# Rows of a source tile's first four blocks taken by one-hot products on TensorE in a graph network's two tile passes

## Chip, cores and metric

One core of a Trainium2 chip runs one program. The metric is the device time of one execution in microseconds, as the median of three runs.

## What is computed

Four graph layers follow each other on 6,250 nodes of 128 numbers and 100,000 edges. The edges come sorted by `dst`, and their `src` is random. The change touches the last two layers, which take the graph the other way round: they sum over `src` and read rows at `dst`.

```python
# third layer: dst = edge_index[0], src = edge_index[1], edge_index = stack([src, dst]);
# h = relu(layernorm(x)) is the feature
feat_n = feature[src] * relation_weight
seg_sum = segment_sum(feat_n, dst, n)
seg_cnt = segment_sum(ones, dst, n)
neigh_mean = seg_sum / maximum(seg_cnt, 1.0)
x = x + concatenate([feature, neigh_mean]) @ W + b
# fourth layer: row, col = edge_index; deg counts row; h = relu(layernorm(x))
agg = segment_sum(deg_inv_sqrt[row] * deg_inv_sqrt[col] * h[col], row, n)
x = x + agg @ W.T + b
```

## The kernel before

A node tile is 128 nodes, and there are T = 49 of them. `edge_layout`, `histogram`, `order_nodes`, `lay_runs` and `place_edges` build the lists for the first two layers. The first layer is four `edge_pass` loops ("attend"), the second one more ("heads"), and in both GpSimd gathers rows with indirect DMAs.

While the first three edge passes run, a sort in their shadow writes the edges to `regions_d` in DRAM: one region for each source tile (`src >> 7`), and in it, edge after edge, one word that packs the table row of `dst` with the place of `src` in its tile, and in a second region the edge's weight. `list2_setup` prepares this sort from edges laid out as [128 partitions x 816 columns] in `so.store`. `place_rest` ends it and leaves in `chunks` how many chunks of 2,176 edges the fullest tile needs, which is one here.

`norm_rows` writes the normalised rows to `table_d` and keeps them in SBUF as `k.q`. Then `tile_pass` runs twice, as "weigh" (third layer) and as "sum" (fourth layer). For each source tile it handles 2,176 edges as GC = 17 columns of 128:

- GpSimd (POOL) issues 17 indirect DMAs, each of which gathers 128 rows into `rows[b]` (L1269). There are RB = 4 such buffers, so it may be up to four tiles ahead of the sums.
- VectorE (DVE) compares `order` (in PSUM) with the edges' places and gets the tile's 17 one-hot matrices (L1366).
- ScalarE (ACT), in the "weigh" pass alone, multiplies each column's rows by the edge weights (L1407). In the "sum" pass the rows are used as they are.
- TensorE (PE) sums the 17 products of one-hot matrix and rows in `total` in PSUM (L1470), which DVE adds to `k.sums` (L1278).

Every eight tiles a group is finished: PE transposes (L1431), multiplies (L1441, L1446, L1451), DVE and ACT normalise, SP stores. Every engine runs its own program in order, and the engines wait for each other's semaphores. The first gather of the "sum" pass needs the last rows that the "weigh" pass stored. SP issues the plain DMAs: the packed lists (L1244) and the stores.

## Time and profile before

| What | us |
|---|---|
| Median of three runs | 11020.37 |
| The three runs | 11018.97, 11020.37, 11024.36 |
| Span of the profiled execution, first to last instruction | 8504.6 |

The profiled execution's own time is not given apart from the runs. The runs' median is 2515.8 us above its span; that part lies around the instructions, where the profile shows nothing. In the span, POOL is busy for 69%, DVE for 42%, PE for 40% and ACT for 26%. The two tile passes take the last 2,143 us of the span. "PEclk" and "granted clock" are the share of TensorE's full clock, 0.50 (1.2 GHz) or 1.00 (2.4 GHz). A float32 matmul stands in the trace as two MATMUL records, so the 17 products of a tile are 34 records. The time of an indirect DMA on POOL is that of writing its descriptors; the transfer comes behind it.

### The profile page before, as it was taken

What the parts mean: (1) busy time and instruction counts of PE and PEld (TensorE: products, weight loads), DVE (VectorE), ACT (ScalarE), POOL (GpSimd) and SP (SyncE); (2) the same over time, 40 slices, a digit from 0 to 9 for tenths busy, and PEclk for the clock granted to TensorE, in tenths of its full rate; (3) what the DMA queues carried; (4) which work ended last, traced back from release to release, by engine and by line L of the source; (5) the groups of instructions that cost most, each with busy time, mean ns of one, the idle gap of its engine ahead of it and who ended that gap; (6) DMA issues with size and microseconds to landing.
All of it is one profiled execution on the core that took longest, in us unless ns stands there. A gap on an engine that the chain in (4) does not pass through costs nothing. (4 is left out here: it accounts for less than half of the span.)

```text
span 8504.6 us, 106528 instructions
## 1 busy us (share of the span) xinstructions
PE 3426.3 (40%) x18282; PEld 3028.2 (36%) x18283; DVE 3575.8 (42%) x13136; ACT 2245.1 (26%) x6884; POOL 5889.8 (69%) x6182
## 2 busy tenths in 40 slices
PE   5434443444434344434333354454542333323333
PEld 4234443444434344434322342333322333323233
DVE  7455553455533555433333355777751111111111
ACT  0212222322223222223222233555532222200000
POOL 0467777577776777766777746777747777677777
PEclk9566666666667666667666677777766666666666
DMA  0322222122221222211222213333322222122222
GB/s 21 93 48 53 54 54 55 42 53 54 53 54 43 51 54 53 54 49 49 54 54 54 55 40 110 105 105 105 105 70 54 55 58 55 53 55 58 55 55 55
DMA packets 374250, 509.70 MB, mean 60 GB/s; under 512 B 217568, under 2 KB 259556, under 8 KB 373796
## 3 DMA queue, kind: packets, MB, share of 16 engines
q0 software_dynamic: 212288, 464.41, 20.5%
q1 hardware_dynamic: 149854, 38.28, 2.1%
q10 hardware_dynamic: 11978, 5.55, 0.3%
q8 instruction: 49, 0.80, 0.0%
q14 instruction: 81, 0.66, 0.0%
HBM read 458.78 MB, written 49.00 MB: 60 GB/s over the span
## 5 line engine op out<-in xcount | busy, mean ns | idle before, releaser
L1625 POOL DMA_INDIRECT rows<-table_d,meta x3200 | 3035.5, 949 | 1013.2 <-issue 894.2
L1685 PE MATMUL ps_total<-weighted_rows,ident 128*128 128x129 f32 (+1 forms) x8000 | 1733.8, 397 | 2495.8 <-ACT weighted_rows L1708 2006.7
L1685 PEld LDWEIGHTS ps_total<-weighted_rows,ident 128*128 128x128 f32 x8000 | 1558.3, 275 | 2665.2 <-issue 2556.5
L1827 DVE SCALAR_TENSOR_TENSOR prod<-rows,q_rows 128x129 f32<-128x129 f32 x3200 | 928.5, 294 | 2120.4 <-DMA rows<-table_d,meta 1584.0
L1470 PE MATMUL tile_sums<-tile_rows,sums 128*128 128x129 f32 x3332 | 609.7, 366 | 1504.8 <-ACT tile_rows L1407 766.4
L1470 PEld LDWEIGHTS tile_sums<-tile_rows,sums 128*128 128x128 f32 x3332 | 592.4, 279 | 1524.5 <-issue 1510.6
L1269 POOL DMA_INDIRECT tile_rows<-table_d,tile_halves x833 | 789.9, 948 | 266.3 <-issue 253.6
L1269 POOL DMA_INDIRECT tile_rows<-rows_d,tile_halves x833 | 789.3, 948 | 265.4 <-issue 253.7
L1708 ACT ACTIVATE weighted_rows<-rows,power 128x129 f32<-128x129 f32 x3200 | 959.4, 389 | 6.5
L1625 POOL DMA_INDIRECT rows<-pairs_d,meta x800 | 774.9, 969 | 257.9 <-issue 243.2
L1702 ACT ACTIVATE power<-expo 128x17 f32<-128x17 f32 x200 | 43.6, 218 | 3020.9 <-DVEq L1860 3020.9
L1278 DVE TENSOR_TENSOR sums<-sums,tile_sums 128x129 f32<-128x129 f32 x98 | 28.4, 290 | 1728.4 <-PE tile_sums L1470 1728.4
L1719 ACT ACTIVATE weighted_rows<-once_weighted,of_relation 128x136 f32<-128x136 f32 x1600 | 484.7, 393 | 191.7 <-DVE once_weighted L1879 190.0
L1407 ACT ACTIVATE tile_rows<-tile_rows,tile_packed 128x128 f32<-128x128 f32 x833 | 248.8, 387 | 787.1 <-DMA tile_rows<-table_d,tile_halves 787.1
L1662 PE MATMUL sort_made<-sort_to_slot,sort_to_tile 128*98 128x80 f32 x1728 | 283.6, 360 | 235.4 <-DVEq L1804 235.4
L1662 PEld LDWEIGHTS sort_made<-sort_to_slot,sort_to_tile 128*98 128x98 f32 x1728 | 274.3, 273 | 245.8 <-DVEq L1804 245.8
L1830 DVE TENSOR_TENSOR src_store<-rows,q_rows 128x128 f32<-128x128 f32 x800 | 211.1, 289 | 257.9 <-DMA rows<-pairs_d,meta 256.7
L1377 ACT COPY sums<-tile_turned 128x1024 f32<-128x1024 f32 (+2 forms) x21 | 18.7, 892 | 1058.0 <-PE tile_turned L1431 1058.0
L1827 DVE DVE_READ_ACCUMULATOR prod<-rows,q_rows 128x1 f32 x3200 | 262.9, 82 | 0.0
L2402 POOL DMA_INDIRECT table_d<-h_rows,perm_in x147 | 147.6, 1004 | 146.0 <-DVE h_rows L2371 102.1
L1366 DVE TENSOR_TENSOR sums<-tile_order,tile_packed 128x2176 f32<-128x2176 f32 x98 | 237.4, 2425 | 12.6 <-DVE x_rows L1319 1.2
L1643 PE MATMUL ps_total<-nothing,ident_bf 128*128 128x129 bf16 (+1 forms) x780 | 105.1, 250 | 312.5 <-issue 226.6
(569 smaller groups left out, 4756.8 us busy)
## 6 DMA issues: line engine op xcount, KB each, us to landing
rows<-table_d,meta POOLq DMA_INDIRECT x3200, 2.5
tile_rows<-table_d,tile_halves POOLq DMA_INDIRECT x833, 2.5
tile_rows<-rows_d,tile_halves POOLq DMA_INDIRECT x833, 2.5
rows<-pairs_d,meta POOLq DMA_INDIRECT x800, 2.8
meta<-list_in_d SPq DMA_DIRECT2D x250, 32.0 KB
words<-words_in_d SPq DMA_DIRECT2D x250, 0.0 KB
resets<-resets_in_d SPq DMA_DIRECT2D x250, 8.0 KB
table_d<-em_h ACTq DMA_DIRECT2D x7, 448.0 KB, 4.7
```

The source lines that it names most:

```text
L1269: pool.indirect_dma_start(rows[b][:, c, 0:P], None, table_d, bass.IndirectOffsetOnAxis(meta[:, t, c:c + 1], 0)).then_inc(got[b] if t < T - ...
L1366: dve.tensor_tensor(spare[:, q], order[:].unsqueeze(1).to_broadcast([P, GC, P]), lane_no[:, t, :].unsqueeze(2).to_broadcast([P, GC, P]), A ...
L1407: ins = act.activation(rows[b][:, c, 0:P], rows[b][:, c, 0:P], ACT.Copy, scale=packed[:, 1, t, c:c + 1])
L1470: mm = pe.matmul(total[:, q, 0:P + 1], spare[:, q, c, :], rows[t % RB][:, c, :], start=(c == 0), stop=(c == GC - 1))
L1625: pool.indirect_dma_start(rows[q][:, j, 0:width], None, table_d, bass.IndirectOffsetOnAxis(meta[q][:, j, number:number + 1], 0)).then_inc( ...
L1662: pe.matmul(placed_ps, to_tile[:, c].rearrange("p r t -> p (r t)"), to_slot[:, c, :], start=(c == 0), stop=(c == SC - 1), skip_group_check ...
L1685: mm = pe.matmul(total[:, q, ds(part, 1), 0:W].rearrange("p a w -> p (a w)"), k.ident[:], wide[:, j % WS, :], start=False, stop=True, skip ...
L1708: ins = act.activation(wide[:, j, :], rows[q][:, j, :], ACT.Copy, scale=power[q][:, 0, j + 1:j + 2])
L1719: ins = act.activation(wide[:, j % WS, r * HW:(r + 1) * HW], once[:, j].rearrange("p h d -> p (h d)"), ACT.Copy, scale=of_relation[q][:, j ...
L1827: own(dve.scalar_tensor_tensor(prod[:, j, :], rows[q][:, j, :], -1.0, asked, ALU.mult, ALU.mult, accum_out=score[:, j, :]))
L1830: own(dve.tensor_tensor(prod[:, j, :], rows[q][:, j, 0:w], asked, ALU.mult))
L2402: pool.indirect_dma_start(k.table_d, bass.IndirectOffsetOnAxis(k.perm[:, t:t + 1], 0), k.h[:, t, :], None).then_inc(m["scattered"], 16)
```

## The change

The first four of the 17 columns of each source tile (its first 512 edges) no longer come from GpSimd. Since edges reach the regions in order of `dst`, the table rows of such a column all lie in a few node tiles, a window: columns 0 to 3 read tiles 0 to 4, 2 to 7, 4 to 10 and 7 to 14. For each of the 5 + 6 + 7 + 8 = 26 node tiles in the windows, DVE makes a one-hot matrix and PE multiplies it with the table's tile in SBUF, 26 float32 products, which leave the column's rows in PSUM (`gathered`). ACT copies them to SBUF ("sum") or weighs them on the way ("weigh"). POOL issues FARC = 13 indirect DMAs instead of 17.

What goes with it:

- `edge_layout` and `histogram` load the edges a second time, in their natural order, straight into `so.store` (six DMAs on SP beside the histogram, in pieces of 64 bytes). `list2_setup` works from these.
- A new stage, `near_edges`, behind `place_rest`, splits the near columns' words into window row and place, and stores both. Edges outside their window would go to a second list, and `sweeps` would then be 2: both tile passes would run all tiles twice.
- The tables must be in SBUF: `k.q` in "weigh", and the rows that "weigh" makes now go to `k.x` instead of the two buffers `made`. What stood in `k.x` is read back from `rows_d` (`residual`, one DMA of all rows). The "sum" pass gathers from a new `made_d`.
- SP loads for each tile the window rows of its 512 near edges, spread over all partitions (`rows_of_window`).

```diff
-PARTS = (0, 6, 11, 15, 17)
+PARTS = (0, 5, 9, 12, 13)
+WINDOWS = ((0, 5), (2, 6), (4, 7), (7, 8))
+NEAR = len(WINDOWS)
+FARC = GC - NEAR
+BATCHES = ((0, 3), (1, 2))
+HOTS = 3
 # GpSimd
-                        for c in range(GC):
+                        for c in range(FARC):
                             pool.indirect_dma_start(rows[b][:, c, 0:P], None, table_d, ...
 # VectorE
+                    def spread_windows(t):
+                        dve.wait_ge(windowed[t % 2], 16 * (t // 2 + 1))
+                        for i, columns in enumerate(BATCHES):
+                            n = len(BATCHES) * t + i
+                            if n >= HOTS:
+                                dve.wait_ge(m["gathered"], n - HOTS + 1)
+                            at = 0
+                            for c in columns:
+                                w = WINDOWS[c][1]
+                                ins = dve.tensor_tensor(near_hot[n % HOTS][:, at:at + w, :], window[t % 2][:, c].unsqueeze(1).to_broadcast([P, w, P]),
+                                                        window_of[:, 0:w].unsqueeze(2).to_broadcast([P, w, P]), ALU.is_equal)
+                                at += w
+                            ins.then_inc(m["near_hot"], 1)
...
+                            if t + 1 < T:
+                                spread_windows(t + 1)
 # ScalarE
                     for t in range(T + 4):
+                        if t < T:
+                            act.wait_ge(m["gathered"], len(BATCHES) * (t + 1))
+                            if t >= 2:
+                                act.wait_ge(m["summed"], t - 1)
+                            taken = gathered[:, 0:NEARP].rearrange("p (c w) -> p c w", w=P)
+                            if weigh:
+                                for c in range(NEAR):
+                                    ins = act.activation(near_rows[q][:, c, 0:P], taken[:, c, :], ACT.Copy, scale=near[:, 1, t, c:c + 1])
+                            else:
+                                ins = act.copy(near_rows[q][:, :, 0:P], taken)
+                            ins.then_inc(m["near_rows"], 1)
                         if weigh and t < T:
-                                act.wait_ge(got[b], (t // RB + 1) * GC * 16)
-                            for c in range(GC):
+                                act.wait_ge(got[b], (t // RB + 1) * FARC * 16)
+                            for c in range(FARC):
 # TensorE
+                    def gather(t):
+                        if t:
+                            pe.wait_ge(m["near_rows"], t)
+                        for i, columns in enumerate(BATCHES):
+                            n = len(BATCHES) * t + i
+                            pe.wait_ge(m["near_hot"], n + 1)
+                            at = 0
+                            for c in columns:
+                                first, w = (WINDOWS if t < T - 1 else WINDOWS_LAST)[c]
+                                for j in range(w):
+                                    mm = pe.matmul(gathered[:, c * P:(c + 1) * P], near_hot[n % HOTS][:, at + j, :],
+                                                   table[:, first + j, 0:P], start=(j == 0), stop=(j == w - 1), skip_group_check=True)
+                                at += w
+                            mm.then_inc(m["gathered"], 1)
...
+                            pe.wait_ge(m["near_rows"], t + 1)
+                            for c in range(NEAR):
+                                pe.matmul(total[:, q, 0:P + 1], spare[:, q, c, :], near_rows[q][:, c, :], start=(c == 0), stop=False)
                             if t < T - 1 and weigh:
                                 pe.wait_ge(m["weighted"], t + 1)
                             elif t < T - 1:
-                                pe.wait_ge(got[t % RB], (t // RB + 1) * GC * 16)
+                                pe.wait_ge(got[t % RB], (t // RB + 1) * FARC * 16)
...
                             mm.then_inc(m["summed"], 1)
+                        if t + 1 < T:
+                            gather(t + 1)
 # near_edges, the engines' work in one turn, shortened
+                    for r in range(2):
+                        sp.dma_start(listed[:, r].rearrange("t c p -> t (c p)"), so.regions_d[r * T:(r + 1) * T, ds(e * CHUNK, NEARP)]
+                                     ).then_inc(m["listed"], 16)
...
+                    own(dve.tensor_copy(whole[:], listed[:, 0]))
+                    own(dve.tensor_scalar(real[:], listed[:, 0], 0.0, None, ALU.is_lt))
...
+                    for c in range(NEAR):
+                        pe.transpose(facts_ps[:, 0, c, 0:T], lane[:, c, :], k.ident[0:T, 0:T])
+                        mm = pe.transpose(facts_ps[:, 1, c, 0:T], listed[:, 1, c, :], k.ident[0:T, 0:T])
...
+                    sp.dma_start(so.near_d[ds(e, 1)].rearrange("a p f -> (a p) f"), facts[:].rearrange("p r t c -> p (r t c)")
+                                 ).then_inc(m["stored"], 16)
+                    sp.wait_ge(m["stored"], 5 * 16)
```

On TensorE in the "weigh" pass, from the fifth source tile on, a tile was one row of 17 products (`tile_sums` is `total`, `tile_turned` and `tile_new` are the group's transposes and products):

```order
L1470 MATMUL tile_sums<-tile_rows_13920,sums 128x129 x17
L1470 MATMUL tile_sums<-tile_rows_13921,sums 128x129 x17
L1470 MATMUL tile_sums<-tile_rows_13922,sums 128x129 x17
L1431 MATMUL tile_turned<-ident,q_rows 128x128 x8
L1470 MATMUL tile_sums<-tile_rows_13923,sums 128x129 x17
L1441 MATMUL tile_new<-bias_parts_3299,ones_bf 128x512 x6
L1446 MATMUL tile_new<-w_3295,sums 128x128 x8
```

The same tiles in the changed kernel (`near_gathered` is `gathered`, `q_rows` the table, and `near_rows` and the window rows lie in `src_store`):

```order
L1698 MATMUL tile_sums<-src_store,sums 128x129 x4
L1708 MATMUL tile_sums<-tile_rows_14218,sums 128x129 x13
L1684 MATMUL near_gathered<-q_rows,near_hot_14225 128x128 x13
L1684 MATMUL near_gathered<-q_rows,near_hot_14226 128x128 x13
L1698 MATMUL tile_sums<-src_store,sums 128x129 x4
L1708 MATMUL tile_sums<-tile_rows_14219,sums 128x129 x13
L1684 MATMUL near_gathered<-q_rows,near_hot_14224 128x128 x13
L1684 MATMUL near_gathered<-q_rows,near_hot_14225 128x128 x13
```

Each tile's 17 products are now in two pieces, and the next tile's 26 gather products stand behind them, ahead of any group work.

On ScalarE in the "weigh" pass, around the first group's transposes, it was:

```order
L1407 ACTIVATE tile_rows_13922<-tile_rows_13922,tile_packed 128x128 x17
L1407 ACTIVATE tile_rows_13923<-tile_rows_13923,tile_packed 128x128 x17
L1377 COPY sums<-tile_turned 128x1024
L1407 ACTIVATE tile_rows_13920<-tile_rows_13920,tile_packed 128x128 x17
L1407 ACTIVATE tile_rows_13921<-tile_rows_13921,tile_packed 128x128 x17
```

And in the changed kernel:

```order
L1626 ACTIVATE tile_rows_14220<-tile_rows_14220,tile_packed 128x128 x13
L1614 ACTIVATE src_store<-near_gathered,src_store 128x128 x4
L1626 ACTIVATE tile_rows_14221<-tile_rows_14221,tile_packed 128x128 x13
L1586 COPY sums<-tile_turned 128x1024
L1614 ACTIVATE src_store<-near_gathered,src_store 128x128 x4
L1626 ACTIVATE tile_rows_14218<-tile_rows_14218,tile_packed 128x128 x13
```

The weighing of a tile's 13 gathered columns now stands behind the four that read what TensorE gathered for the same tile.

On VectorE, per tile, one comparison of 2,176 elements became two of together 2,176, followed by four that make the next tile's window matrices:

```order
L1571 TENSOR_TENSOR sums<-tile_fixed,src_store 128x512
L1573 TENSOR_TENSOR sums<-tile_fixed,tile_packed 128x1664
L1548 TENSOR_TENSOR near_hot_14225<-src_store,tile_fixed 128x640
L1548 TENSOR_TENSOR near_hot_14225<-src_store,tile_fixed 128x1024
L1548 TENSOR_TENSOR near_hot_14226<-src_store,tile_fixed 128x768
L1548 TENSOR_TENSOR near_hot_14226<-src_store,tile_fixed 128x896
```

`tile_fixed` is in PSUM and holds both `order` and `window_of`; the other operand is in SBUF.

## Rows read from the trace of the kernel before

**Rows 1.** The page: the span, and each engine's busy time, share and instructions.

```profile
span 8504.6 us, 106528 instructions
PE 3426.3 (40%) x18282; PEld 3028.2 (36%) x18283; DVE 3575.8 (42%) x13136; ACT 2245.1 (26%) x6884; POOL 5889.8 (69%) x6182
```

**Rows 2.** The chain that ended last, from 7300 us on: share by line.

```profile
by line: POOL tile_rows L1269 65.3%; issue 21.1%; DMA tile_rows<-rows_d,tile_halves 0.2%; DMA tile_packed<-list_out_d 0.2%; PE tile_new L1451 0.1%; PE tile_sums L1470 0.1%; POOLq L1239 0.1%; PE tile_new L1441 0.1%; PE tile_turned L1431 0.1%
```

**Rows 3.** Line 1269: instructions (ns min/median/max, first and last start us) and idle.

```profile
L1269 POOL DMA_INDIRECT tile_rows<-table_d,tile_halves x833: 941/947/1561, 6375.3 to 7417.9; - x167
L1269 POOL DMA_INDIRECT tile_rows<-rows_d,tile_halves x833: 940/947/1569, 7449.0 to 8490.9; - x167
  issue: 507.3, 1664
```

**Rows 4.** Waits of the whole span: who waited, us, times, longest.

```profile
PE tile_sums L1470 <- ACT tile_rows L1407: 766.4, 50, 92.3
PE tile_sums L1470 <- DMA tile_rows<-rows_d,tile_halves: 738.5, 52, 43.3
```

**Rows 5.** Timeline of a tile in "weigh": start, us, engine, line, count, idle before.

```profile
6716.83 5.07 ACT L1407 ACTIVATE tile_rows<-tile_rows,tile_packed 128x128 f32<-128x128 f32 x17 [15.92 <-DMA tile_rows<-table_d,tile_halves]
6721.81 0.99 ACT L1377 COPY sums<-tile_turned 128x1024 f32<-128x1024 f32 x1
6722.04 5.67 PE L1470 MATMUL tile_sums<-tile_rows,sums 128*128 128x129 f32 x34 [14.20 <-ACT tile_rows L1407]
```

**Rows 6.** Timeline of PE at the start of a tile's products.

```profile
6701.05 4.13 PE L1470 MATMUL tile_sums<-tile_rows,sums 128*128 128x129 f32 x18 [15.05 <-ACT tile_rows L1407]
```

**Rows 7.** Windows: us, busy of PE, PEld, DVE, ACT, POOL, PEclk, DMA, GB/s.

```profile
6701.00:6704.90 3.90, 3.85 (x18) 3.88 (x19) 0.00 (x0) 0.00 (x0) 2.99 (x4) 0.50 0.23 61
6729.00:6730.00 1.00, 1.00 (x9) 0.96 (x9) 1.00 (x2) 0.00 (x0) 0.69 (x2) 1.00 0.23 66
```

**Rows 8.** Timeline of "weigh" around a group's work on DVE and PE.

```profile
6728.64 1.23 DVE L1311 TENSOR_TENSOR sums<-sums,tile_inv 128x1024 f32<-128x1024 f32 x1
6729.05 2.05 PE L1446 MATMUL tile_new<-w,sums 128*128 128x128 f32 x16
6729.37 1.31 POOL L1269 DMA_INDIRECT tile_rows<-table_d,tile_halves  x1 [0.30 <-issue]
6729.78 2.42 DVE L1366 TENSOR_TENSOR sums<-tile_order,tile_packed 128x2176 f32<-128x2176 f32 x1
6730.99 0.94 POOL L1269 DMA_INDIRECT tile_rows<-table_d,tile_halves  x1 [0.30 <-issue]
```

**Rows 9.** Timeline of ACT and DVE in the layer turn: work on 512 columns.

```profile
5001.62 0.57 ACT L2306 COPY lt_ht<-lt_rows 128x512 f32<-128x512 f32 x1
5000.26 0.69 DVE L2384 TENSOR_TENSOR x_rows<-x_rows,lt_out 128x512 f32<-128x512 f32 x1
```

**Rows 10.** Timeline of `place_rest`: its first and last steps, and the next stage's first.

```profile
5010.85 0.48 PE L1050 MATMUL rest_turned<-ident,sort_base 98*1 98x98 f32 x2 [2.29 <-PEq L94]
5015.63 1.87 DVE L1102 MEMSET rest_blank<- 98x2176 f32 x1 [2.13 <-DVEq L1104]
5023.82 0.15 DVE L1127 CAST rest_idx<-rest_place 128x1 int32<-128x1 f32 x1 [3.75 <-DMA list_out_d<-sort_lane]
5039.90 0.53 POOL L2493 MEMSET hw_mix<- 128x512 f32 x1 [8.75 <-DMA list_out_d<-rest_rec,rest_idx]
```

**Rows 11.** Lines from 0 to 175 us (busy us, mean ns): the histogram's products.

```profile
L256 PE MATMUL hist_count<-oh 128*128 128x49 bf16 x784 | 90.0, 277 | 14.5 <-DVE oh L226 14.5
```

**Rows 12.** DMA issues: count, KB each, median us to landing.

```profile
x_rows<-rows_d SPq DMA_DIRECT2D x7, 448.0 KB, 6.7
tile_packed<-list_out_d SPq DMA_DIRECT2D x28, 59.5 KB, 3.3
```

More of the change, by code:

```diff
@@ L1206, in tile_pass @@
         if weigh:
-            made = [buf(nc, s, f"tile_made{q}", [P, TG, P]) for q in range(2)]
             stats = buf(nc, s, "tile_stats", [P, TG, 6])
@@ L1220, in tile_pass @@
         parts = k.parts2 if weigh else k.parts3
+        table = k.q if weigh else k.x
         turns = nc.values_load(chunks[0:1, 0:1], min_val=1, max_val=CHUNKS)
+        again = nc.values_load(sweeps[0:1, 0:1], min_val=1, max_val=2)
         TURNS_OF = 2 if weigh else 1
@@ L1237, in _ @@
                     dve.memset(rows[b][:, :, P:P + 1], 1.0)
-        with nc.Fori(0, turns) as e:
+                for q in range(2):
+                    dve.memset(near_rows[q][:, :, P:P + 1], 1.0)
+        with nc.Fori(0, turns) as e, nc.Fori(0, again) as again_i:
             with nc.Block() as block:
```

258 lines of the change are left out of this document (210 added, 48 removed).

## The prediction

> **What bounds the kernel now.** I read the page first: no engine is busy throughout, but POOL is far ahead with 69% [rows 1]. Then I asked the chain that ended last for the stretch of the two tile passes. The reader is to see there that nearly all of it is POOL's line 1269 and the "issue" behind it [rows 2]: one indirect DMA after another, with 0.3 us between them. So the passes last as long as POOL needs for its gathers. Line 1269's own view gives the pace [rows 3]: 833 gathers start from 6375.3 to 7417.9 us in "weigh" and from 7449.0 to 8490.9 us in "sum", that is 1042.6 / 832 = 1.253 us and 1041.9 / 832 = 1.252 us each. A tile of 17 costs 21.3 us. It hardly ever waits for anyone else: the idle time of the two passes is 507.3 us of "issue" in 1664 pieces, which is the 0.3 us that belongs to each gather. The waits say the same from the other side [rows 4]: PE stands idle some 15 us per tile, for ACT in one pass (766.4 us) and for the DMA in the other (738.5 us). What a change is worth here is read from POOL's count of gathers, as long as no other loop gets longer than POOL's.
>
> **What is removed.** 4 x 49 = 196 gathers a pass, 392 in all. At 1.253 us that is 245.6 us a pass, **-491 us** in all. POOL's tile then takes 13 x 1.253 = 16.3 us.
>
> **What takes its place, and whether it hides under 16.3 us.** This is the step that I chose most carefully, because in "weigh" the new work closes a ring. PE gathers tile t+1 only behind the sums of tile t; ACT can weigh the 13 gathered columns of t+1 only behind the four that PE's products left in PSUM; and PE can sum the 13 only when ACT is done. In the order above these stand behind each other on either engine. So one tile of "weigh" costs, whatever POOL does:
>
> - on PE 13 sums and 26 gather products, 39 float32 products or 78 records. At half clock a stretch of 3.90 us held 18 records, 3.85 us of work, so 0.214 us each [rows 7]. At full clock 16 records took 2.05 us, 0.128 us each with the tail of the last [rows 8], and a microsecond touches nine; I take 0.12.
> - on ACT 4 + 13 columns: 17 took 5.07 us [rows 5]. The four come out of PSUM; I price them alike.
> - three hand-offs: ACT ended at 6721.90 and PE began at 6722.04, 0.14 us each [rows 5], 0.4 us.
>
> At full clock throughout this is 9.4 + 5.5 = 14.9 us; at half clock 16.7 + 5.5 = 22.2 us. Which of the two? In the trace PE comes out of 15 us of idle, does 18 records in 4.13 us at half clock [rows 6], and is at full clock afterwards [rows 7, 8]. In the new loop a burst is 78 records long and the pause before it is some 5 us, with four sums (8 records) inside it. If each burst still begins cold, it is 18 x 0.214 + 60 x 0.12 = 11.1 us, and the ring 16.6 us. I take this value, since PE still pauses in each tile: 0.3 us over POOL's 16.3, times 48 tiles, **+15 us**. The ends are 14.9 us (POOL paces, +0) and 22.2 us (+289). The group's own products stand behind the next tile's gather, where PE waits for ACT's 5 us anyway, and ACT's group work (0.99 us for a copy of 1,024 columns [rows 5]) lies under PE's burst: nothing.
>
> In "sum" ACT weighs nothing. The ring is 86 records and one copy of 512 columns, 0.57 us [rows 9], with 0.3 us of hand-offs: 11.2 us at full clock, 3.9 + 68 x 0.12 + 0.9 = 13.0 us when each burst begins cold, 19.3 us at half clock. I take 13.0: POOL paces, nothing is lost. Its bad end is (19.3 - 16.3) x 49 = +147 us.
>
> DVE adds 3,328 compared elements a tile in four instructions. 2,176 took 2.42 us [rows 8], so 3.7 us; with the old comparison and the add it is about 6.7 of 16.3 us. Its window matrices are made a tile ahead in three buffers. If this cover were gone they would stand in the ring at 3.7 us a tile. They could also disturb POOL. The trace shows both sorts: while L1311, with both inputs in SBUF, ran, a gather took 1.31 instead of 0.94 us, and beside L1366, with one input in PSUM, it took 0.94 us [rows 8]. The new ones have one input in PSUM (`window_of`), so I price this at nothing.
>
> [...]
>
> **SP's queue.** Window rows for tile t are fetched as soon as the matrices of t-2 are made, a tile before they are used; a fetch like it takes 3.3 us to land [rows 12], against 16 us. The residual is 3.2 MB; a seventh of it takes 6.7 us to land [rows 12], seven one behind the other at most 47 us. The window rows of tile 2 queue behind it. POOL reaches the end of tile 1 only 33 us into the pass and has four buffers, so this delays at most the second or third tile, once: I take +1 us, and 14 as its end. The stores stand in SP's program six tiles after their group and hold nothing up. Extra constants at each pass's start, 1 us each. Together **+3 us**.
>
> **The new stage.** The trace has no such stage; its nearest relative is `place_rest`, which from 5010.85 to 5039.90 us did 29 us of small steps with two waits for writes to DRAM, of which the last cost 8.75 us [rows 10]. For `near_edges` I count: fills on POOL, one of 3,328 columns (2,176 took 1.87 us [rows 10], so 2.9 us) and some eighteen small ones, 8 us; the lists, 3.3 us; 14 DVE steps of 512 columns at 0.69 us [rows 9], 9.7 us; transposes and their copy, 2 us; the last store and its wait, 8.75 us; the reduction and the barriers of three blocks, 5 us. **+37 us**, ends 20 and 60.
>
> **Nothing for the rest.** The six loads in natural order are 18,750 pieces of 64 bytes. A packed list is 896 pieces of 68 bytes (59.5 KB) and lands in 3.3 us, and 28 of them were loaded without anyone waiting long [rows 12]; the new ones are as much as 21 of them, at worst 69 us one after the other, and lie beside the histogram, whose products alone take 90.0 us [rows 11]. `list2_setup` does three DVE steps fewer but waits for its blank store as before.
>
> **Sum.** -491 + 15 + 3 + 37 = -436 us. It is made against the profiled execution: its span of 8504.6 us becomes 8069 us. Its time apart from the runs' median of 11020.4 us isn't given; I keep the 2515.8 us around the span as they are, and get 10584 us.
>
> **Rivals.**
>
> *TensorE's ring paces.* If PE runs colder than I take it, "weigh" goes to 22.2 us a tile at worst and "sum" to 19.3: 10584 - 15 + 289 + 147 = 11005 us. For it: all of PE's bursts now begin at half clock, and the ring is already equal to POOL's pace. Against: bursts get more than twice as long and pauses three times shorter. A middle case, 0.18 us a record (half the records cold), gives 14.0 + 5.5 = 19.5 us in "weigh" alone, +157 instead of +15: 10726 us.
>
> *DVE's comparisons hold up POOL.* As worked out from the 1.31 us row: 0.36 us for a 1.23 us instruction, so 1.1 us a tile, +106 us, 10690 us; at worst 363 us, 10947 us. Against it is the 0.94 us row.
>
> *The part around the span moves too.* The profile says nothing of these 2515.8 us. If they went with the span, they would shrink by 436 x 2515.8 / 8504.6 = 129 us, 10455 us; if they went with what the program allocates in DRAM, which grows by two more sets of regions and the new tables, they would grow, by a sum that I can't bound from the trace.
>
> *Slower: a second sweep.* One edge outside its column's window is enough for `sweeps` to be 2, and then both passes run all 49 tiles again: 2 x (798 + 31) = 1658 us (31 us lie between the last gather of "weigh" and the first of "sum" [rows 3]), 12242 us. The order within a region decides it, and whether it is truly the order of `dst`. I counted the reference's edges by source tile in that order: all 49 x 512 lie in their windows, and the fullest tile has 2,168 of 2,176 places. So I hold it unlikely. It is also the case in which the change would not do what it says.
>
> **How the numbers follow.** As forecast, POOL or an equal ring pacing, 10540 to 10640 us: 0.63. A colder ring, 10640 to 10900: 0.16. DVE disturbing POOL: 0.04. The part around the span shrinking, 10440 to 10510: 0.07; growing: 0.06, half of it beyond the gain. Second sweep: 0.04. The range from 10510 to 10700 holds the first case, the cheaper half of the second and third, both ends of the new stage. A difference of 0.2%, 22 us, is about what can be told from none here. Faster by more: 0.92; within: 0.02; slower: 0.06 (second sweep, half of the growth, less what overlaps).
>
> **What would show it.** The gather line should have 637 instructions a pass, still 1.25 us apart, and about 798 us from first to last in "sum". In "weigh" POOL should start to wait for PE's sums late in the pass if the ring is longer than 16.3 us; the granted clock of a burst shows which end was right. The port rival would show as gathers over 1 us beside the window comparisons. `near_edges` should last 37 us. The prediction is wrong if "weigh" spans more than 900 us, if the gathers double, or if time and span no longer differ by 2516 us.

## The result, and the profile after

The changed kernel took 10827.82 us (median of four runs, 10819.31 to 10837.80) beside 11022.37 us of the kernel before (four runs, 11018.97 to 11025.45): ratio 0.9826, 95% interval 0.9812 to 0.9840. It is 195 us faster, and I had forecast 436. The cause came out when both kernels ran beside each other on other chips. The forecast's gain was measured on one chip and not on the four others, and by its time the profile of before belongs to the first kind, the timed runs to the second. One execution of the variant e2_again took 10756 us where its four others took 10559 to 10593, and its median below is that of the four.

The page of the changed kernel, the lines that answer to [rows 1]:

```profile
span 10817.6 us, 117700 instructions
PE 4633.8 (43%) x23388; PEld 3788.7 (35%) x23389; DVE 3961.6 (37%) x13646; ACT 2271.5 (21%) x6933; POOL 5523.9 (51%) x5814
```

This execution took 10819.71 us. Its span is 2 us shorter, not 2,516. So nothing lies "around" the instructions: here the 2,516 us are in the span. This was one of the prediction's own signs of being wrong; "weigh" over 900 us, below, is a second. The gathers' line, which answers to [rows 3]:

```profile
L1455 POOL DMA_INDIRECT tile_rows<-table_d,tile_halves x637: 941/947/1306, 8648.8 to 9734.9; - x160
L1455 POOL DMA_INDIRECT tile_rows<-made_d,tile_halves x637: 941/947/1508, 9811.5 to 10772.6; - x160
...
  PE tile_sums L1708: 429.7, 73
  issue: 360.4, 1182
```

There are 637 gathers a pass as forecast, each as long as before (947 ns), but "weigh" lasts 1086.1 us from the first to the last and "sum" 961.1 us, not 798. POOL waits 429.7 us for PE's sums, of which there was nothing in the profile of before. What PE is late for is seen in the timeline of one tile in "sum":

```profile
10316.29 5.97 PE L1684 MATMUL near_gathered<-x_rows,near_hot 128*128 128x128 f32 x52
10319.40 1.95 DVE L1548 TENSOR_TENSOR near_hot<-src_store,tile_fixed 128x768 f32<-128x768 f32 x2 [8.42 <-PE near_gathered L1684]
...
10326.49 0.59 ACT L1616 COPY src_store<-near_gathered 128x512 f32<-128x512 f32 x1 [16.96 <-DMA rows<-table_d,meta]
10326.57 1.95 DVE L1548 TENSOR_TENSOR near_hot<-src_store,tile_fixed 128x640 f32<-128x640 f32 x2 [2.39 <-DMA rows<-table_d,meta]
...
10327.22 2.06 PE L1698 MATMUL tile_sums<-src_store,sums 128*128 128x129 f32 x8 [4.96 <-issue]
```

PE's 52 records end at 10322.26. ACT and DVE, which wait for them alone, start at 10326.49 and 10326.57, some 4.2 us late and at the same moment. (The named releaser is a guess of the profile: that line had issued its last gather 3,800 us earlier.) Over "weigh" this hand-off, from the end of PE's gather burst to ACT's start, has a median of 5.2 us; I had priced each of the three at 0.14. Summed over the 49 tiles of "weigh" these hand-offs take 328 us, and in the trace of a0_fifth (next section) 1.9 us. The gather bursts themselves take 306 us here and 297 there, so it is the hand-off and not the new products that got long.

### The profile page after: what moved, and what is told of

It reads as the page before. It is cut to its first block and busy times, and to the rows that moved or that the text cites. A ratio compares the mean times of both kernels' runs of the same rounds, so it can differ in the third digit from the quotient of the medians.

```text
span 10817.6 us, 117700 instructions
## 1 busy us (share of the span) xinstructions
PE 4633.8 (43%) x23388; PEld 3788.7 (35%) x23389; DVE 3961.6 (37%) x13646; ACT 2271.5 (21%) x6933; POOL 5523.9 (51%) x5814
## 5 line engine op out<-in xcount | busy, mean ns | idle before, releaser
L1925 PE MATMUL ps_total<-weighted_rows,ident 128*128 128x129 f32 (+1 forms) x8000 | 2267.6, 436 | 4384.2 <-issue 3355.9
L1455 POOL DMA_INDIRECT tile_rows<-table_d,tile_halves x637 | 603.8, 948 | 495.3 <-PE tile_sums L1708 303.0
L1548 DVE TENSOR_TENSOR near_hot<-src_store,tile_fixed 128x640 f32<-128x640 f32 (+3 forms) x392 | 381.4, 1016 | 1240.1 <-issue 487.7
L1455 POOL DMA_INDIRECT tile_rows<-made_d,tile_halves x637 | 604.4, 949 | 370.0 <-issue 180.2
L1698 PE MATMUL tile_sums<-src_store,sums 128*128 128x129 f32 x784 | 180.2, 402 | 632.8 <-issue 377.0
L1698 PEld LDWEIGHTS tile_sums<-src_store,sums 128*128 128x128 f32 x784 | 156.2, 295 | 652.4 <-issue 652.4
L1684 PE MATMUL near_gathered<-x_rows,near_hot 128*128 128x128 f32 x2548 | 337.0, 291 | 75.5 <-issue 74.8
L1684 PEld LDWEIGHTS near_gathered<-x_rows,near_hot 128*128 128x128 f32 x2548 | 322.3, 207 | 85.6 <-issue 85.3
L1684 PE MATMUL near_gathered<-q_rows,near_hot 128*128 128x128 f32 x2548 | 299.0, 278 | 74.6 <-issue 74.6
L1684 PEld LDWEIGHTS near_gathered<-q_rows,near_hot 128*128 128x128 f32 x2548 | 295.4, 195 | 75.0 <-issue 74.9
```

What stands on the lines that cost most here:

```text
L1455: pool.indirect_dma_start(rows[b][:, c, 0:P], None, table_d, bass.IndirectOffsetOnAxis(meta[:, t, c:c + 1], 0)).then_inc(got[b] if t < T - ...
L1548: ins = dve.tensor_tensor(near_hot[n % HOTS][:, at:at + w, :], window[t % 2][:, c].unsqueeze(1).to_broadcast([P, w, P]), window_of[:, 0:w] ...
L1684: mm = pe.matmul(gathered[:, c * P:(c + 1) * P], near_hot[n % HOTS][:, at + j, :], table[:, first + j, 0:P], start=(j == 0), stop=(j == w ...
L1698: pe.matmul(total[:, q, 0:P + 1], spare[:, q, c, :], near_rows[q][:, c, :], start=(c == 0), stop=False)
L1925: mm = pe.matmul(total[:, q, ds(part, 1), 0:W].rearrange("p a w -> p (a w)"), k.ident[:], wide[:, j % WS, :], start=False, stop=True, skip ...
```

## The same two kernels on the other kind of chip

The page, the gathers and the windows of the changed kernel (a0_fifth) on a chip where the kernel before takes 8,499 us:

```profile
span 8032.8 us, 117700 instructions
PE 3989.1 (50%) x23388; PEld 3571.6 (44%) x23389; DVE 3953.1 (49%) x13646; ACT 2268.3 (28%) x6933; POOL 5509.4 (69%) x5814
```

```profile
L1455 POOL DMA_INDIRECT tile_rows<-table_d,tile_halves x637: 940/944/1739, 6395.9 to 7190.8; - x160
L1455 POOL DMA_INDIRECT tile_rows<-made_d,tile_halves x637: 940/944/1289, 7225.4 to 8019.9; - x160
...
  issue: 387.7, 1272
```

POOL hardly waits for anything but its own 0.3 us, as before the change. Windows of the two passes, columns as in [rows 7] (stretch, its length, PE, PEld, DVE, ACT, POOL, granted clock, DMA share, GB/s):

```profile
6395.90:7190.80 794.90, 613.22 (x4466) 591.57 (x4467) 353.63 (x495) 265.66 (x878) 601.11 (x636) 0.85 0.29 77
7225.40:8019.90 794.50, 606.41 (x4360) 585.47 (x4361) 336.41 (x384) 34.56 (x55) 600.66 (x636) 0.84 0.28 73
```

The kernel before on such a chip (b0_again), its gathers:

```profile
L1269 POOL DMA_INDIRECT tile_rows<-table_d,tile_halves x833: 941/947/1562, 6382.4 to 7425.8; - x167
L1269 POOL DMA_INDIRECT tile_rows<-rows_d,tile_halves x833: 941/947/1983, 7457.1 to 8502.2; - x167
```

From these and the two spans (8515.9 and 8032.8) the difference comes apart:

| Stretch | before, us | changed, us | difference | my term |
|---|---|---|---|---|
| up to the first tile gather | 6382.4 | 6395.9 | +13.5 | +37 |
| "weigh", first to last gather | 1043.4 | 794.9 | -248.5 | -245.6 + 15 |
| between the passes | 31.3 | 34.6 | +3.3 | +3 in all |
| "sum", first to last gather | 1045.1 | 794.5 | -250.6 | -245.6 |
| last gather to end | 13.7 | 12.9 | -0.8 | 0 |
| sum | | | -483.1 | -436 |

The medians are 8499.39 and 8036.40 us, -463 us. (The profiled execution of b0_again took 8517.4.)

What the kinds of chips differ in shows in register steps, the address and counter arithmetic that an engine's own program does between its instructions ("DVEq" for VectorE's), shortest/median/longest in ns. First the kind of a0_fifth, then that of the first comparison, the same line of the same program:

```profile
L2067 DVEq ALU_OP  x6400: 40/45/52, 494.1 to 4914.6; - x194
L2067 DVEq FUSED_REGOPS  x3200: 67/67/80, 494.3 to 4914.7; - x189
```

```profile
L2067 DVEq ALU_OP  x6400: 2/45/1424, 507.8 to 6540.8; - x194
L2067 DVEq FUSED_REGOPS  x3200: 2/67/1424, 508.1 to 6540.9; - x189
```

The median is the same, but there are stretches in which a step takes 0.70 us. In the first comparison's trace I count 5,926 of 34,962 register steps at 0.4 us or more, together 4,290 us: 2,894 on DVE, 2,954 on PE, 78 on SP, none on ACT or POOL; in that of b0_again and a0_fifth not one. They come in phases, as from 994.6 to 1029.2 us, in which DVE and PE are slow from and to the same moment. I call this the crawl. The same line also shows where most of the time lies: the four "attend" passes end their products at 4914.6 us on the one, at 6540.8 on the other, 1,626 of the 2,785 us between the two spans of the changed kernel.

## Experiments

Each group has its own runs of the kernel before on the same chip, so ratios and differences are taken within a group. Groups A and E ran on one and the same chip, 40 minutes apart, without the crawl both times; B, C, D and F ran on four different chips, all with it. So the kind without the crawl is known from one chip, and from the first profile of before. A single run has no ratio.

| Group | before, us | kernel | us | ratio (95%) |
|---|---|---|---|---|
| A | 8497.24 | b0_again (one run) | 8517.44 | |
| | | e1_window_late | 8037.23 | 0.9459 (0.9443 to 0.9474) |
| | | e2_far_first | 8041.54 | 0.9464 (0.9448 to 0.9480) |
| B | 11007.78 | a0_again | 10835.56 | 0.9837 (0.9820 to 0.9853) |
| | | port_window_sbuf | 10916.61 | 0.9914 (0.9893 to 0.9935) |
| | | ring9_near_first | 10665.76 | 0.9689 (0.9669 to 0.9708) |
| | | b13_gathers_only | 10489.53 | 0.9528 (0.9509 to 0.9548) |
| C | 10858.17 | b0_third (one run) | 10856.04 | |
| | | a0_third | 10606.98 | 0.9772 (0.9756 to 0.9788) |
| | | e2_again | 10568.26 | 0.9732 (0.9716 to 0.9748) |
| | | e1_again | 10581.08 | 0.9747 (0.9727 to 0.9766) |
| D | 10992.82 | a0_fourth | 10813.44 | 0.9840 (0.9823 to 0.9856) |
| | | port_again | 10896.55 | 0.9908 (0.9890 to 0.9926) |
| | | ring9_again | 10637.02 | 0.9676 (0.9657 to 0.9695) |
| | | two_tiles_a_column | 10683.66 | 0.9715 (0.9698 to 0.9731) |
| E | 8499.39 | a0_fifth | 8036.40 | 0.9455 (0.9440 to 0.9471) |
| F | 10980.12 | port_third | 10864.73 | 0.9886 (0.9865 to 0.9906) |
| | | ring9_third | 10612.74 | 0.9664 (0.9645 to 0.9684) |

**The kernel before again** (no edit; b0_again, b0_third).

> The kernel before, unchanged, profiled once more. Theory A (the 2,516 us lie inside the program in ordinary executions, and the first profile was an execution without them): span about 11,019 us, time about 2 us above it; the four edge passes of the first layer last some 2,200 us longer than in the first profile, and DVE's and PE's register steps take some 700 ns in phases there, as in the changed kernel's profile. Theory B (they lie around the span and only the changed kernel's own code brings them inside): span about 8,505 us again, time 2,516 us above it. In either case the stage times of this profile, set beside the changed kernel's, tell in which stage the measured 195 us were gained.

> The kernel before, profiled once more. If the kernel before takes about 11,010 us on this chip, then by Theory A its profile has the span of about 11,008 us, some 5,900 register steps of 700 ns, edge passes that end some 2,200 us later than in the first profile, and tile passes of about 2,410 us instead of 2,133. If it takes about 8,500 us, none of that: span 8,500 us.

In group A the span was 8,515.9 us, but the time too was 8,517: neither theory had foreseen that the runs themselves would be 2,500 us shorter. In group C the span was 10,854.5 us with 5,674 slow register steps of 34,835. There the two theories part, and the first one holds: the extra time lies inside the program. The gathers of the tile passes in b0_third:

```profile
L1269 POOL DMA_INDIRECT tile_rows<-table_d,tile_halves x833: 938/944/1667, 8434.3 to 9606.7; - x167
L1269 POOL DMA_INDIRECT tile_rows<-rows_d,tile_halves x833: 938/944/1760, 9654.7 to 10823.3; - x167
...
  DMA em_x<-in_x: 137.5, 20
  remote: 124.7, 18
```

Even the kernel before does not keep POOL's pace there: 1172.4 us for "weigh" instead of 1043.4. Some 262 us of idle time come in 38 pieces, each at the start of a tile, where POOL waits only for sums of four tiles back. (The names are again guesses: no such DMA is waited for there.) The timeline of b0_third has the cause, PE's products and POOL's gathers:

```profile
8587.28 0.94 POOL L1269 DMA_INDIRECT tile_rows<-table_d,tile_halves  x1 [0.30 <-issue]
8588.19 0.38 PE L1470 MATMUL tile_sums<-tile_rows,sums 128*128 128x129 f32 x1 [2.42 <-issue]
...
8589.59 0.29 PEld L1470 LDWEIGHTS tile_sums<-tile_rows,sums 128*128 128x128 f32 x1 [2.51 <-issue]
...
8590.99 0.38 PE L1470 MATMUL tile_sums<-tile_rows,sums 128*128 128x129 f32 x1 [2.42 <-issue]
...
8601.48 11.65 PE L1470 MATMUL tile_sums<-tile_rows,sums 128*128 128x129 f32 x80 [1.02 <-issue]
...
8602.39 0.94 POOL L1269 DMA_INDIRECT tile_rows<-table_d,tile_halves  x1 [9.18 <-DMA em_x<-in_x]
```

For 59 us PE does little more than one load or one matmul every 1.40 us, waiting for nothing that the profile shows ("issue"); POOL gets four tiles ahead and stands for 9.18 us. Then PE does 80 records in 11.65 us and POOL goes on. So the crawl is not confined to register steps, and the buffers hide most of it, but not all.

**The changed kernel again** (no edit; a0_again, a0_third, a0_fourth, a0_fifth).

> The changed kernel itself, unchanged, once more beside the kernel before. In the first comparison the kernel before took 11,022 us, in the last one 8,497 us, on another chip. Theory A (the 2,516 us are register steps of some 700 ns on VectorE and TensorE, which a chip has or has not, and they also stretch the ring in the tile passes): where the kernel before takes about 8,500 us this one takes about 8,040 us, ratio 0.946, with gathers of a pass 796 us from first to last and no gap behind PE's gather; where it takes about 11,020 us this one takes about 10,825 us, ratio 0.983. Theory B (the changed kernel's fetch of the window rows costs 5 us a tile on any chip, and the kernels with the late fetch or the far columns first cured that): 8,300 us beside 8,497 us, ratio 0.98.

> The changed kernel itself beside the kernel before. If before takes about 11,010 us: 10,835 us again, ratio 0.983. If before takes about 8,500 us: Theory A (the changed kernel loses its 5 us a tile on that kind of chip alone) 8,040 us, ratio 0.946; Theory B (its order of instructions costs 5 us a tile on any chip, and the two variants cured that) 8,300 us, ratio 0.98.

> The changed kernel itself beside the kernel before. Where before takes about 10,860 to 11,010 us (register steps of 0.70 us in the profile, TensorE at one step per 1.4 us in stretches): ratio 0.977 to 0.984 again. Where before takes about 8,500 us (no such steps), Theory A (the new TensorE work is hidden under POOL's 16.3 us on such a chip): 8,040 us, ratio 0.946, a gain of 460 us beside my 436. Theory B (its order of instructions costs on any chip): 8,300 us, ratio 0.98.

> The changed kernel itself beside the kernel before, on whatever chip comes next. Where before takes about 8,500 us: Theory A (the new work is hidden under POOL's 16.3 us a tile where no step takes 0.70 us) 8,040 us, ratio 0.946; Theory B (its own order costs 5 us a tile on any chip) 8,300 us, ratio 0.98. Where before takes 10,860 to 11,010 us: ratio 0.977 to 0.984 as in the comparisons so far.

Groups B and D repeated the first comparison (172 and 179 us), C gave 251 us, and E gave 463 us: Theory A. The hand-off behind PE's gather has a median of 0.04 us in a0_fifth, 5.9, 2.9 and 5.3 us in a0_again, a0_third and a0_fourth ("weigh").

**The fetch of the window rows a step later** (e1_window_late, e1_again).

```diff
-                            sp.wait_ge(m["near_hot"], len(BATCHES) * (t - 1))
+                            sp.wait_ge(m["near_rows"], t - 1)
```

> The changed kernel with SP's fetch of the window rows issued one tile step later (behind ACT's four near columns instead of behind DVE's window matrices), so that no DMA of SP is issued within 1 us of the end of PE's gather. Theory A (the 5.2 us between the end of PE's last gather product and ACT's and DVE's start come from this fetch): the gap falls to about 0.2 us, the tile of weigh from 21.1 to about 16.5 us, the two passes from 2,169 to about 1,750 us, time about 10,400 us. Theory B (the gap belongs to PE's semaphore write and not to the fetch): gap and time stay, 10,800 to 10,850 us.

> The late fetch of the window rows. Where before takes 8,500 us: 8,037 us again. Where before takes 11,010 us: if the fetch that SP issues 0.8 us before the end of PE's gather makes the hand-off late, the 5.9 us go and it takes about 10,450 us; if not, 10,835 us as the changed kernel.

In the first comparison's trace SP issues this fetch 0.5 to 1 us ahead of the end of PE's gather in 75 of the 92 tiles with a late hand-off. In group A the gap was gone, but from a0_fifth too, so that said nothing. In group C, where it could tell, the fetch went out 11 us or more ahead, and the kernel took 10581 us (two runs) beside 10607: the hand-off's median is 2.3 us beside 2.9. The fetch is not the cause of the late hand-off; the 26 us are all that it could be worth.

**Far columns first** (e2_far_first, e2_again). On PE the 13 products stand ahead of the four near ones, and on ACT the 13 weighings ahead of the four:

```diff
-                            pe.wait_ge(m["near_rows"], t + 1)
-                            for c in range(NEAR):
-                                pe.matmul(total[:, q, 0:P + 1], spare[:, q, c, :], near_rows[q][:, c, :], start=(c == 0), stop=False)
...
+                            pe.wait_ge(m["near_rows"], t + 1)
+                            for c in range(NEAR):
+                                mm = pe.matmul(total[:, q, 0:P + 1], spare[:, q, c, :], near_rows[q][:, c, :], start=False, stop=(c == NEAR - 1))
```

> The changed kernel with the order in the ring turned round: PE sums a tile's 13 gathered columns first and the 4 near ones last, and ACT weighs the 13 ahead of the 4. Then ACT's weighing and PE's 13 sums lie beside the end of the gather's hand-off instead of behind it. Theory A (the ring is what POOL waits for, 21.1 us of which 5.2 are the gap): the ring of weigh falls to about 8.5 (gather) + 5.2 (gap) + 1.3 + 1.9 = 15 to 16 us, POOL paces with 16.3 us, the passes last about 1,750 us and the time is about 10,400 us. Theory B (PE's gap grows with whatever PE does next, or POOL waits for something else): the tile stays at 20 to 21 us and the time within 10,800 to 10,850 us.

> The far columns first, near ones last. Where before takes 8,500 us: 8,040 us again. Where before takes 11,010 us: if the late hand-offs behind PE lie in the ring of the changed kernel (weigh 22.3 us a tile where POOL needs 16.3), this order takes ACT's 13 columns and PE's 13 sums out of the ring, which then has some 16 us; POOL paces more of the time and it takes about 10,620 us. If every hand-off behind PE is late whatever the order, 10,800 us or more.

In A it takes what the changed kernel takes in E (8041.5 and 8036.4 us), since POOL paces. In C it is 39 us faster than the changed kernel, not the 200 that an opened ring should give. So the order in the ring is worth 0.4% there at most, of which the late fetch, with the old order, had 26 us as well, and the best kernel that I found is no more than that ahead. That the gain stayed away also means that taking ACT's and PE's 13 columns out from behind the late hand-off does not free POOL; no run here shows why.

**The removal alone** (b13_gathers_only): the kernel before with 13 gathers a tile.

```diff
-                        for c in range(GC):
+                        for c in range(13):
                             pool.indirect_dma_start(rows[b][:, c, 0:P], None, table_d, ...
```

> The kernel before with 13 instead of 17 gathers a tile (the last four columns of a tile hold old rows; nothing takes their place). It gives the price of the removal by itself: by my term 392 x 1.253 = 491 us less than before, 8,497 - 491 = 8,006 us where before takes 8,497 (10,531 where before takes 11,022, if the removal is worth as much there). If the passes were bound by something else behind POOL, less than that.

It took 518 us less. The removal is worth its full term even on a chip with the crawl, so what is lost there is lost to what was added: 10835.56 - 10489.53 = 346 us, against my 55. The gathers of this run and of a0_again, on the same chip, show where:

```profile
L1269 POOL DMA_INDIRECT tile_rows<-table_d,tile_halves x637: 938/944/1546, 8597.1 to 9507.1; - x160
L1269 POOL DMA_INDIRECT tile_rows<-rows_d,tile_halves x637: 938/944/1757, 9559.3 to 10462.7; - x160
```

```profile
L1455 POOL DMA_INDIRECT tile_rows<-table_d,tile_halves x637: 938/944/1267, 8637.1 to 9753.3; - x160
L1455 POOL DMA_INDIRECT tile_rows<-made_d,tile_halves x637: 938/944/1882, 9831.0 to 10797.2; - x160
```

With the same 637 gathers a pass, "weigh" is 206 us longer (1116.2 beside 910.0), where I had +15, and "sum" 63 us longer (966.2 beside 903.4), where I had nothing. Up to the first tile gather it is 40 us, where I had +37, and between and behind the passes 45 us, where I had 3.

**The ring by itself** (ring9_near_first, ring9_again, ring9_third): four more gathers a tile left out, so that POOL needs 11.3 us.

```diff
-                        for c in range(FARC):
+                        for c in range(9):
                             pool.indirect_dma_start(rows[b][:, c, 0:P], None, table_d, ...
```

> The changed kernel with only 9 of the 13 far columns of each tile gathered (the other four hold old rows; ACT, PE and DVE work on all as before), so that POOL needs 11.3 us a tile and the ring of the other engines shows its own length. My price of the ring was 16.6 us in weigh, with ends 14.9 (full clock) and 22.2 (half clock), and 13.0 us in sum: then weigh lasts 49 x 16.6 = 813 us and sum 49 x 13.0 = 637 us. If the ring is at full clock throughout, 730 us and 549 us. If it were the half-clock ring, weigh would last 1,088 us and POOL would have been waiting in the changed kernel as well.

> Nine of 13 far gathers a tile, the rest of the work as in the changed kernel. Where before takes 11,010 us, weigh lasted 1,025 us and sum 853 us from the first to the last gather, the ring with TensorE's crawl in it. Where before takes 8,500 us: my price of the ring, 16.6 us in weigh and 13.0 us in sum, gives 813 and 637 us; a ring at full clock 730 and 549 us.

> Nine of 13 far gathers a tile, all other work as in the changed kernel. Where before takes 8,500 us: POOL no longer paces and the ring shows its length. My price, 16.6 us in weigh and 13.0 us in sum, gives 813 and 637 us from the first to the last gather, a ring at full clock throughout 730 and 549 us, at half clock 1,088 and 946 us. Where before takes about 11,000 us: 1,020 and 850 us again.

All three fell on chips with the crawl. The gathers of ring9_again:

```profile
L1455 POOL DMA_INDIRECT tile_rows<-table_d,tile_halves x441: 938/944/1323, 8625.6 to 9645.1; - x147
L1455 POOL DMA_INDIRECT tile_rows<-made_d,tile_halves x441: 938/944/1541, 9734.7 to 10581.1; - x147
...
  PE tile_sums L1708: 792.8, 90
```

1019.5 us in "weigh" and 846.4 in "sum", some 21 and 17 us a tile, whatever POOL does: the ring is longer than POOL's 16.3 us in both passes. Four gathers fewer (5.0 us a tile, 491 us in all) brought only 176 us over a0_fourth. The ring's length without the crawl was not measured alone; the timeline of a0_fifth has it where PE does not wait for a DMA:

```profile
6910.68 5.97 PE L1684 MATMUL near_gathered<-q_rows,near_hot 128*128 128x128 f32 x52
...
6916.69 1.14 ACT L1614 ACTIVATE src_store<-near_gathered,src_store 128x128 f32<-128x128 f32 x4 [11.10 <-PE near_gathered L1684]
...
6917.70 3.90 ACT L1626 ACTIVATE tile_rows<-tile_rows,tile_packed 128x128 f32<-128x128 f32 x13
...
6921.66 3.17 PE L1708 MATMUL tile_sums<-tile_rows,sums 128*128 128x129 f32 x26 [2.55 <-ACT tile_rows L1626]
...
6924.66 5.97 PE L1684 MATMUL near_gathered<-q_rows,near_hot 128*128 128x128 f32 x52
```

From one gather's start to the next 13.98 us, at 0.115 and 0.122 us a record in the two bursts.

**Fewer products in the gather** (two_tiles_a_column).

```diff
-                                for j in range(w):
+                                for j in range(2):
```

> The changed kernel with 8 instead of 26 gather products a tile on TensorE (two node tiles a column; the others' rows are left out), everything else as it is. TensorE then has 21 float32 products a tile, 84 steps with the weight loads, instead of 39 and 156. Theory A (on the chips with the crawl the new work is paid by TensorE's steps): there the stalls of POOL nearly vanish and about 250 us of the changed kernel's time go, 10,585 where it takes 10,835; where before takes 8,500 us nothing changes, 8,040 us. Theory B (what is paid there is the hand-off and not the number of steps): less than 80 us of gain on such a chip.

It took 130 us less than a0_fourth, where Theory A had 250 and Theory B under 80. With 18 of 26 products gone the hand-off stayed late (its median 5.0 us in "weigh", 9.8 in "sum"), and POOL still waited 254.5 us for PE's sums. The trace says where the rest went: in "sum" the gather bursts take 151 us instead of a0_fourth's 364, but the hand-offs behind them 540 instead of 287, and PE's bursts follow each other every 20.7 us in the one and 20.6 in the other. In "weigh" the tile falls from 23.5 to 21.3 us. So the hand-off is no fixed price per tile: in "sum" it grew by more than the products that were left out.

**Both inputs of the window comparisons in SBUF** (port_window_sbuf, port_again, port_third).

```diff
-        order, window_of = fixed[:, 0:P], fixed[:, P:P + 8]
+        order, window_of = fixed[:, 0:P], window_no
```

> The changed kernel with window_of in SBUF, so that DVE's window comparisons have both inputs in SBUF. By the row of the kernel before (0.36 us more for a gather beside 1.23 us of L1311) 1.1 us a tile are added to POOL's 16.3, about 105 us in all: 8,145 us where the changed kernel takes 8,040. [...] If the placement does not matter: 8,040 us, gathers of a pass 796 us.

> window_of in SBUF, so that the window comparisons have both inputs there. [...]

> window_of in SBUF. [...] Where before takes about 11,000 us: 83 us more than the changed kernel again.

It cost 81 us in B and 83 in D, all three on chips with the crawl. Timeline of port_again:

```profile
9209.46 0.94 POOL L1454 DMA_INDIRECT tile_rows<-table_d,tile_halves  x1 [0.30 <-issue]
9209.63 1.96 DVE L1547 TENSOR_TENSOR near_hot<-src_store,window_no 128x768 f32<-128x768 f32 x2 [10.79 <-issue]
9210.71 1.70 POOL L1454 DMA_INDIRECT tile_rows<-table_d,tile_halves  x1 [0.30 <-issue]
9212.72 0.94 POOL L1454 DMA_INDIRECT tile_rows<-table_d,tile_halves  x1 [0.30 <-issue]
```

The gather that starts under the comparisons takes 1.70 us instead of 0.94. The one that starts 0.17 us ahead of them keeps its 0.94 us, and so does the next. All 1,274 gathers are busy for 1,298 us, beside 1,205 in a0_fourth, 94 us more; my row of 1.31 us had given 106. In all, 158 gathers start under a window comparison, and they take 1.54 us on average and at most 1.99; all others take 0.95, so these 158 make up the 94 us. The comparisons' whole length, 400 us, is not what it costs. In a0_fourth, with one input in PSUM, 274 gathers start under one and take 0.94 us.

The Trainium skill (SBUF — State Buffer, "Who interferes with whom") has it that a VectorE instruction with two SBUF inputs contends with a GpSimd instruction that reads SBUF, and not with one that only writes it; of `tensor_tensor` it infers that writing descriptors is not held up. The trace agrees that one input in PSUM costs nothing. With both in SBUF a gather, which writes descriptors and reads its row numbers from `tile_halves`, is held up, 1.54 instead of 0.94 us, so the measurement decides against that inference for an indirect DMA.

## Why the prediction was wrong, point by point

**The base: the step that failed, and the term that it made wrong.** "I keep the 2515.8 us around the span as they are." The span of before (8,504.6 us) fits the one kind of chip and its timed runs (11,020 us) the other, and I put the difference outside the program. In every run shown since, time and span differ by 1 to 3 us. A sum of durations from a trace without the crawl was thus added to a time that has 2,516 us of it. The base alone does not move the number, since 11020 - 436 is 10584 wherever those 2,516 us lie. What it let through are the hand-offs at 0.14 us each, and with them the ring's term, +15 us in "weigh" and nothing in "sum": on a chip with the crawl the same two passes lost 206 and 63 us, and some 45 us between and behind them where I had 3. Against its own kind the sum is off by less: 8504.6 - 436 = 8069 us forecast for the span, 8032.8 us measured. Of the 47 us between the table's -483 and -436, 15 are the ring's, 9 the new stage's, 8 the removal's and 15 come from earlier passes that were shorter in that execution.

**The removal.** 491 us forecast; 499 us between first and last gathers of the two passes on a chip without the crawl, 518 us alone on one with it. Right on both.

**The ring in "weigh".** Priced at 16.6 us a tile, with 14.9 at full clock as one end. Without the crawl it takes 13.98 us and POOL paces, so +15 us was 0. I had taken each burst to begin at half clock, 18 records of it. In a0_fifth that holds for the 13 far sums alone and not for the gather: behind their pause the sums' 26 records take 4.81 us in the median tile of "weigh" (granted clock 0.67 on average over such bursts), and the gather's 52 behind them 5.97 us, 0.115 us each (0.99). In the tile of 13.98 us the sums too ran at full clock, 3.17 us; with 4.81 the ring is 15.6 us, still under POOL's 16.3. With the crawl, in the first comparison, "weigh" took 1086.1 us, 22.2 us a tile, and "sum" 961.1 us, 19.6 us a tile. These are nearly the 22.2 and 19.3 us of my half-clock ends, by coincidence: the windows of the first comparison's trace show a granted clock of 0.74 and 0.79, not 0.50.

```profile
8648.80:9734.90 1086.10, 634.27 (x4206) 604.87 (x4206) 344.91 (x479) 252.28 (x838) 602.90 (x637) 0.74 0.22 57
9811.50:10772.60 961.10, 608.22 (x4095) 581.41 (x4096) 327.12 (x369) 32.03 (x51) 603.41 (x637) 0.79 0.24 60
```

The gather bursts ran at 0.98. The tile is long for the most part because of the hand-off, 328 us in "weigh" instead of 1.9. The clock pays a smaller part: the sums' 26 records take 5.14 us in the median, at 0.61, instead of 3.17. So "TensorE's ring paces" is the rival that came true on those chips, by a mechanism that it did not name; 10827.8 us lies between its 10726 and its 11005, which is luck, since both were reckoned from the clock.

**DVE and POOL.** Right. The comparisons last 4.1 us a tile (3.7 forecast), and beside them a gather takes 0.94 us. The price if the placement had been the other was 94 us of gathers and 81 to 83 us of time on chips with the crawl, forecast 106. The rival's worst case of 363 us is the comparisons' whole length; only the gathers that start under one pay.

**SP and the passes' starts.** +3 us forecast, +3.3 us between the passes.

**The new stage.** +37 us forecast. Its first instruction and the next stage's first, in a0_fifth:

```profile
L1214 POOL MEMSET window_first<- x4: 92/108/122, 5033.1 to 5033.2; 49x1 f32 x4
```

```profile
L2733 POOL MEMSET hw_mix<- x1: 529/529/529, 5061.4 to 5061.4; 128x512 f32 x1
```

28.3 us, and 28.3 us also in a0_third, with the crawl. It is inside the range of 20 to 60; the small steps overlapped more than I allowed. What the table shows up to the first tile gather is 13.5 us, since the earlier passes were 15 us shorter in that execution.

**The part around the span.** As a rival it falls too, since there is no such part. But what I had put there does move. In group C the "heads" pass, whose code the change does not touch, took 1532.6 us from first to last gather in a0_third and 1468.5 in b0_third: 64 us lost in a stretch that I had priced at nothing. In group B it is 28 us (1563.8 in a0_again, 1535.9 in b13_gathers_only). These are single executions, and that it comes from where the slow phases fall is not shown.

**The second sweep.** It did not happen: 637 gathers a pass.

**What stays open.** What makes DVE, PE and SP step at 0.70 us on some chips and in some stretches, whether it would be there if the execution were not recorded, and what releases the late hand-off. It tends to come with the end of one of the gathers' 4-byte packets (within 30 ns for 53% of the late ones in the first comparison's trace, 33% for moments drawn at random from the same waits), which is no proof. The ends of PE's records are modelled, so a late signal and a late end of the products can't be told apart either. No run here takes the crawl away on a chip that has it. The ring by itself and the placement of `window_of` were not measured without it, and the chip without it is a single one.

## What to carry to other kernels

Before a sum is made, set the profiled execution's span against the timed runs: if they differ by more than the microseconds that every run shows, treat them as of two kinds of chips until a second profile says otherwise: the profile's waits and hand-offs do not price the timed runs, though most of its durations may. Read a gain from work taken off a pacing engine as far as the next ring, and ask what that ring costs when each hand-off in it takes microseconds instead of 0.14 us: the slack between a ring of 14.0 to 15.6 us a tile and POOL's 16.3 was enough on one kind of chip and not on the other. A kernel is then worth comparing on both.

## What the runs showed of the hardware that I had not expected

The kernel before takes 8,500 us on one chip and 10,860 to 11,020 us on others, and repeats its time within 0.3% on the same one. On the latter DVE's and PE's steps take 0.70 us in stretches (PE then one load or matmul per 1.40 us), while ACT's weighing of 17 columns (5.07 us), the gathers on POOL (944 ns) and their 4 KB packets (211 ns, b0_again and b0_third) keep their durations. ACT and DVE start late there behind PE's gather, by a median of 2.9 to 5.9 us in the changed kernel and 1.0 to 1.3 us with `window_of` in SBUF (where the long ones among them make up for it: 613 us over both passes in port_again, 621 in a0_fourth). A DVE comparison with both inputs in SBUF lengthened a gather that started under it from 0.94 to 1.54 us on average; with one input in PSUM it did not at all.
